# Unread products in TensorE's four pauses at the seam of attention and mixing

## The reference

```
x: (2, 2048, 512)   ctx: (2, 77, 512)   16 heads of 32
x = layernorm(x + attn(x, w_qkv, w_out) + b_out)
x = layernorm(x + softmax(x @ ctx.T / sqrt(32)) @ ctx @ xW_out.T)
x = layernorm(x + down(quant(silu(gate(xq)) * up(xq))))
```

## Time and profile before

| | |
|---|---|
| median of 3 runs | 1835.33 us (1834.75 to 1836.08) |
| the profiled execution | 1834.5 us |
| its span, first to last instruction | 1832.7 us |
| TensorE busy | 1789.0 us, 98% of the span |
| VectorE busy | 1454.8 us, 79% |
| ScalarE busy | 1448.8 us, 79% |
| mean granted TensorE clock | 0.991 |

### The profile page before, as it was taken

The page is one execution under the profiler, slowest core; times in us unless marked ns, Lnnn a source line. Parts: engine busy times, 40 slices in busy tenths (PEclk is TensorE's granted clock), DMA queues, the critical chain, the costliest instruction groups (busy, mean ns, idle before and its releaser), DMA issues. The chain is left out here.

```text
span 1832.7 us, 40393 instructions
## 1 busy us (share of the span) xinstructions
PE 1789.0 (98%) x16160; PEld 907.0 (49%) x16186; DVE 1454.8 (79%) x1582; ACT 1448.8 (79%) x1580; POOL 156.2 (9%) x144
## 2 busy tenths in 40 slices
PE   8999998999999999999999999999979999999997
PEld 7887884333333333333333333333337776644443
DVE  5444346889899898898998989989974777788798
ACT  5344356999999999999999999999955555456487
POOL 0000002000000000000000000000012221000054
PEclk9999999999999999999999999999999999999998
DMA  8665655536447346355464463554456440132075
GB/s 299 218 224 202 213 199 167 111 79 170 99 96 170 93 99 167 82 136 131 97 146 116 93 171 86 110 157 101 93 143 204 144 137 24 60 130 126 1 293 206
DMA packets 106370, 256.32 MB, mean 140 GB/s; under 512 B 8180, under 2 KB 24692, under 8 KB 96756
## 3 DMA queue, kind: packets, MB, share of 16 engines
q1 hardware_dynamic: 97012, 187.08, 28.6%
q0 software_dynamic: 9216, 67.11, 19.7%
HBM read 105.01 MB, written 82.05 MB: 102 GB/s over the span
## 5 line engine op out<-in xcount | busy, mean ns | idle before, releaser
L895 DVE TENSOR_TENSOR dve_sum<-dve_sum,probs 128x2048 f32<-128x2048 f32 x320 | 737.5, 2305 | 11.2 <-ACT probs L816 1.4
L816 ACT ACTIVATE probs<-score_others,shift_now 128x1536 f32<-128x1536 f32 x384 | 597.7, 1557 | 0.0
L981 PE MATMUL mixed_ps<-probs,value_piece 128*32 128x512 f32 (+1 forms) x3840 | 408.7, 516 | 1.1 <-ACT probs L816 0.2
L815 ACT ACTIVATE probs<-score_first,shift_now 128x512 f32<-128x512 f32 x384 | 266.5, 694 | 3.9 <-PE score_others L948 1.1
L948 PE MATMUL score_first<-first_queries,key_piece 32*128 32x512 f32 x768 | 246.0, 425 | 5.5 <-ACT probs L815 3.0
L948 PE MATMUL score_others<-first_queries,key_piece 32*128 32x512 f32 x2304 | 248.6, 426 | 0.0
L948 PE MATMUL score_others<-q_second,key_piece 32*128 32x512 f32 x2304 | 247.2, 424 | 0.0
L948 PE MATMUL score_first<-q_second,key_piece 32*128 32x512 f32 x768 | 245.0, 424 | 0.2
L948 PEld LDWEIGHTS score_first<-first_queries,key_piece 32*128 32x128 f32 x768 | 122.0, 183 | 185.0 <-ACT probs L815 84.0
L948 PEld LDWEIGHTS score_first<-q_second,key_piece 32*128 32x128 f32 x768 | 121.9, 183 | 184.1 <-ACT probs L815 100.9
L816 ACT ACTIVATE probs_paired<-score_others,shift_now 128x1536 f32<-128x1536 f32 x128 | 198.3, 1549 | 0.0
(11 more groups left out here) (238 smaller groups left out, 2565.5 us busy)
## 6 DMA issues: line engine op xcount, KB each, us to landing
probs_paired<-probs_paired POOLq DMA_DIRECT2D x64, 1024.0 KB, 8.0
o_scratch<-out_parts SPq DMA_DIRECT2D x33, 512.0 KB, 3.1
k_scratch<-parts SPq DMA_DIRECT2D x32, 512.0 KB, 4.2
q_scratch<-parts SPq DMA_DIRECT2D x32, 512.0 KB, 2.7
key_piece<-k_scratch SPq DMA_DIRECT2D x32, 512.0 KB, 5.2
h_scratch<-h SPq DMA_DIRECT2D x5, 2816.0 KB, 8.1
h<-h_scratch SPq DMA_DIRECT2D x5, 2816.0 KB, 11.2
v_scratch<-values SPq DMA_DIRECT2D x32, 256.0 KB, 2.0
```

What stands on the lines that cost most here:

```text
L815: nc.scalar.activation(block_probs(k)[:, 0:CH], score_first[:], ACT.Exp, bias=shift[:, c:c + 1], scale=SCALE).then_inc(probs_done, 1)
L816: nc.scalar.activation(block_probs(k)[:, CH:HPG * CH], score_others[n % 2][:], ACT.Exp, bias=shift[:, c:c + 1], scale=SCALE).then_inc(prob ...
L895: nc.vector.tensor_tensor(total[:], first[:], block_probs(k)[:], ALU.add).then_inc(dve_added, 1)
L981: last = nc.tensor.matmul(mixed_ps[j * HD:(j + 1) * HD, lo:hi], v_group[k // KPP][:, k % KPP, j * HD:(j + 1) * HD], block_probs(k)[:, j * ...
```

## The change

Four groups of products whose result nothing reads are added, 64 products in all, each with a tile of ones as its weights. Nothing is removed. Twelve stand ahead of the last sums of `attend`, eighteen between these sums and the products that turn the extremes, eighteen behind those, still inside the block of `attend`, and sixteen of 77 columns at the start of `mix`, ahead of the load of `wide` on TensorE. The first three groups write to the second half of the score tiles, whose last reader is done; the fourth to the score tile of `mix`.

```
+                def idle(count):
+
+                    for _ in range(count):
+                        nc.tensor.matmul(score_others[1][:, 0:P], keep.ones[:], keep.ident[:], start=True, stop=True)
+
+                idle(12)
                 for at in range(len(TO_SUMS) + 1):
                     sums(CHUNKS, at)
 
+                idle(18)
                 pe.wait_ge(col_done, 2)
                 for side in range(2):
                     last = nc.tensor.matmul(mixed_ps[0:1, side * P:(side + 1) * P], extremes_col[:, side:side + 1], keep.ident[:],
                                             start=True, stop=True)
                 last.then_inc(extremes_row_done, 1)
+                idle(18)
...
+                for _ in range(16):
+                    nc.tensor.matmul(score_ps[:, 0, :], keep.ones[:], keep.ident[:, 0:CTX], start=True, stop=True)
                 with pe.If(pe.value_load(keep.wide[0:1, 0:1], min_val=0, max_val=1) == 0):
                     whole()
```

## The result

The change makes the kernel slower by 0.15%: 1838.14 us median of 16 runs (1836.17 to 1839.98) against 1834.78 us for the kernel before (16 runs, 1832.61 to 1838.01), ratio 1.0015, 95% interval 1.0009 to 1.0022. By the ratio that is 2.8 us, between 1.7 and 4.0; the medians themselves are 3.4 us apart. The prediction was +1.95 us and 1837.3 us.

A forecast was written before the change was run, and what follows sets the result against it. The prediction saw the loss at the seam into `mix`, where TensorE pauses and its clock falls to 0.50. +3.0 + 1.75 - 2.8 = +1.95 us on a median of 1835.33 gave 1837.3 us, range 1834.9 to 1839.4.

The forecast's parts named there:

- The clock's return: First 48 products of `mix`: at full clock they take 11.0 us instead of 13.80, a gain of 2.8 us.
- The third group holds the barrier: End of `attend`: the barrier waits for TensorE's unread products, releasing all engines at 1371.2 instead of 1368.2, +3.0 us.
- The first group delays the sums: Last sums of `attend`: the third sum, and VectorE's chain from the sums to `wide`, come 0.4 us later.
- The second group is hidden by `divide`: Row products of the extremes: 1.4 us late, hidden by VectorE's `divide`; cost nothing, 0.5 us of cover left.
- The fourth group: Start of `mix`: flag test runs beneath the products; release to first product 3.7 us instead of 1.95, +1.75 us.
- C: Start of `mix`: load of `wide` waits until the array is empty; +3.95 us in all, 1839.3 us; chance 0.15.
- D: Barrier ending `attend`: it does not wait for the third group; release at 1368.6, time 1837.0 us; chance 0.03.
- E: At the seam: clock falls despite the products; no 2.8 us gain, +4.75 to +8, 1840 to 1843 us; chance 0.07.
- B: End of `mix`: the low clock there goes away, winning at most 1.7 us; +0.25, 1835.6 us; chance 0.15.

The follow-up runs named there:

- experiment 3: The fitted kernel: the change with 7, 9, 11 and 8 products in its groups instead of 12, 18, 18 and 16; 1832.36 us, ratio to before 0.9983.
- experiment 6: The kernel of experiment 3 without its third group (7, 9, none and 8 products); 1835.65 us, ratio to before 1.0001.
- experiment 4: The change without its first and second groups, third (18) and fourth (16) kept; 1837.22 us, ratio to before 1.0010.
- Experiment 8: The change with 30 products in the second group instead of 18, and no third group; one run, 1838.65 us.
- experiment 2: The change with 8 products in the fourth group instead of 16; 1836.19 us, ratio to before 1.0002.
- experiment 9: The change with 32 products in the fourth group instead of 16; one run, 1842.79 us.
- experiment 1: The change without its third group, the 18 products ahead of the barrier; 1837.91 us, ratio to before 1.0011.
- experiment 5: The change with its third group doubled, 36 products instead of 18; 1841.10 us, ratio to before 1.0034.
- experiment 7: The kernel of experiment 3 without the last six unread products of `mix`; 1831.07 us, ratio to before 0.9981.

## Why the prediction was right, step by step

**The clock's return** (forecast -2.8, measured -2.73). Right, and shown from both sides: experiment 3 keeps every working product's start and gains 2.73 us at the seam; experiment 6 takes the third group away, the clock falls, and 2.53 us of it are lost again. One thing was judged too lightly: that the clock stays because the longest pause is short. It fell in experiment 4 after pauses of 1.6 and 2.5 us with the sums between, and in experiment 6 within one of 3.06 us. In the earlier trace rows the clock had survived the pause of 1.62 us, and that was no proof for a kernel that has a second one.

**The third group holds the barrier** (forecast +3.0). The mechanism is shown: without the group the seam is 3.10 us shorter, with twice the group 4.02 us longer, and SyncE's arrival, 12.5 us behind the value products, does not move with it. This is the term that was mis-sized: the release came 3.82 us later relative to the value products, not 3.0. I had counted whole groups at 0.112 us a record and nothing for the change from one kind of product to the other. The timeline has the difference in pieces: the first group starts 0.99 us behind the value products where I had 0.87, and takes 2.88 us to the pair sums (2.7); the sums between them take another 0.1 us more; the second group takes 4.22 from its start to the row products (4.0); the third takes 4.3 from its start to the end of the drain (4.2), starting another 0.1 late. The extra 0.1 to 0.2 us stand at each passage between the narrow products of the attention (32 rows of output, eight records of 512 columns in 1.07 us, where eight of the full ones in `mix` would take 1.82) and those over the whole array; that the passage is the reason is read from the rows alone and was not tried by itself. With 3.82 the sum would have been +2.8, the middle of the measured interval.

**The first group delays the sums** (forecast 0.4). VectorE's L908 came 11.60 us behind the value products, before 10.90: 0.7, for the same reason. It cost nothing, since the barrier waited for TensorE anyway.

**The second group is hidden by `divide`** (forecast: nothing, cover 0.5 us). Nothing it was, with a cover of 0.2 us: the row products ended at 1366.85 and L908 began at 1367.05. Experiment 8 shows the limit: 12 products more put L908 behind the row by 2.43 us of waiting, one for one. The second group still lengthened the way to the barrier, because the third stands behind it in the queue; that was in the sum.

**The fourth group** (forecast +1.75, measured +1.72). Right, with its mechanism: the test runs beneath the products (experiments 2 and 9), and eight products less are 1.78 us less at the seam, their own length of 16 records. With eight, 1.9 us pass from the release to the first product, as before the change.

**The rivals.** C, a load that waits for an empty array, is refuted by experiments 2 and 9. D, a barrier that does not wait, by experiments 1 and 5. E did not happen in the change itself, whose mean clock was 0.991 to 0.995 in its 16 runs; it happened in experiments 4 and 6, where a group was missing. B, the low clock at the end of `mix`: it stood there in every profiled execution. The stretch that it lies in was 0.5 us shorter after than before and varied by 1.5 us among the kernels; it adds to the scatter between runs and does not explain a slower kernel. The case against B, that executions of the kernel before lie within 1.3 us, rested on three runs; sixteen lie within 5.4 us.

**Where luck helped the number.** The forecast of the median stood on three runs, whose median of 1835.33 us is 0.55 above that of the sixteen, 1834.78. That made up for part of the 0.85 us by which the shift at the seam was too small, so 1837.3 came nearer to 1838.14 than the shift deserved.

**What stays open.** Why the median of experiment 1 fell by less than its seam, while experiment 6 lost the whole gain. The pauses at the barrier were of 1.40 and 3.06 us in their profiled executions, with the clock at 1.00 behind the first and at 0.50 behind the second; no kernel between them was run, and no further execution of experiment 1 was profiled. Whether the last six products of `mix` are worth removing is not settled by experiment 7.

## What to carry to other kernels

Products that keep TensorE's clock up are worth having where a pause is followed by work at half speed, and each group has its own budget: the wait that it fills. Read from the trace how long the releaser takes, fill a little less than that, and count what stands behind the group in the queue; a barrier counts as a wait for the last product. Here 64 products lost 2.8 us and 35, at the same four places, won 3. And do not save on the group that seems idle: without the 11 products ahead of the barrier the whole gain was gone.

## What the runs showed of the hardware

TensorE's queue ran ahead of the array by a constant amount. The load of the flag began 1.61 us behind the first of 32 records (the change), 5.2 us behind the first of 64 (experiment 9), and together with the first of 16 (experiment 2). At 0.112 us a record that leaves 17 or 18 records not yet begun in the first two cases, and as many weight loads. The Trainium skill, "TensorE: Matmul & The Clock Gate", in the table at its head, gives 64 entries. These runs show about 35, if an entry is what the trace shows as a record. The drains of TensorE behind a third group of 11 to 36 products took 2.17 us each, the length of 19 records, much the same.

The load of the flag into a register took 1.03 us before and 1.02 in the fitted kernel, and 0.49 us on the same engine in experiments 2 and 9 and in the change, where it came later. The store of the last rows had by then landed in these three, and was in flight in the first two. That this is the reason was not tried, and experiment 1 does not fit it well: there the load took 0.49 us from 1372.55 on, and the store landed only at about 1373.0. It made no difference to the time, since the products covered both.
